# Output projection of a cross attention: the first two groups' values and the weight blocks change places

## The chip, the cores and the metric

The kernel runs on one core of a Trainium2 chip. The metric is the time on the device, in microseconds, as the median of several executions. TensorE (PE) multiplies matrices, VectorE (DVE), ScalarE (ACT) and GpSimd (POOL) work on rows, and SyncE (SP) issues every DMA of this kernel from one queue, in program order.

## The reference, cut to what matters

The reference is one transformer layer with cross attention, self attention and a feed-forward part, in float32. This case is about the end of the cross attention: the heads' outputs (`out`) times `w_o`, plus the bias and the residual, over 2048 rows. The self attention that comes next uses `w_attn` and `w_proj`.

```
out = jnp.einsum('bhij,bhjd->bhid', attn, v)
out = out.transpose(0, 2, 1, 3).reshape(B, Sq, INNER)
return out @ w_o + b_o
...
x = x + _L0_xattn_ref(_layernorm(x, axis=-1), ctx_768, ...)
x = x + _L0_attn_ref(_layernorm(x, axis=-1), L0_attn_w_attn, L0_attn_w_proj, L0_attn_decay_raw)
```

## The kernel before

Products are made in near float32 precision: every factor is split into a high part (a rounding copy, on ACT) and a low part (the factor minus its high part, on DVE or POOL), and each product is three matmuls (high by high, high by low, low by high). So every factor needs its two splits before TensorE can use it.

The 64 sequences are worked in eight groups (`NG`). For each group the attention leaves its values in `o_dram`. When the last sequence has been mixed, TensorE projects the values of group 7 (four steps, `project_values`; ACT copies half of each, `half_value`, DVE adds the other half, `whole_value`, SP stores them, `store_values`). Meanwhile the output projection is made ready. Its parts, which the steps below name, are these:

- `load_out(g)` on SP loads the values of group g, 1 MB, into `o_in[g % 2]`; `high_out` (ACT, L524) and `low_out` (DVE, L529; for half of group 0 POOL) split them into `os_[g % 2]`, in four pieces for each group.
- `load_block(k)` on SP loads weight block k into one of four raw buffers (`w_raw`); `high_block` (ACT, L502) and `low_block` (DVE, L506) split it. Blocks 0 to 7 are `w_o` (the last two, 6 and 7, are split at the end of the attention), blocks 8 to 23 are the weights of the self attention. A load waits until the block that had its buffer is split: from block 12 on, `load_block(k)` waits for `low_block(k - 4)`, and everything behind it in SP's queue waits too.
- TensorE makes two row tiles of each group, 16 in all, 24 matmuls of 128x512 each, into three banks in turn (the accumulate at L1015). The first waits for all eight `w_o` blocks (`w_lo`) and for the split values of its group.
- DVE adds each product to the rows that POOL has given the bias (L801, L1403), and takes their moments (L1405, L1407).
- For the first four row tiles the next stage's norm is made ahead: ACT takes the square root (`ahead.norm.root`, behind the group's `high_block`s in group 2), DVE finishes it beside row tile 4, POOL scales row tile 0, 1, 2, 3 behind the bias of row tiles 5, 7, 9, 11, and TensorE turns them (`ahead.norm.turn`, L167) behind row tiles 6, 8, 10, 12. ACT and DVE split what was turned (L173, L178; on ACT behind the `high_block`s of its group). All four share one bank: a turn waits for the low split of the one before.

`later(g)` names the four blocks whose loads go with group g. Every engine's program is a hand-written order; the compiler moves nothing.

Of the kernel before, what the change touches and what calls it, by code (L numbers as in the profile page):

```python
# [28 lines left out]
DMA = 16  # L29
# [185 lines left out]
def cross_attention(nc, kept, stack, ident, ident_ready, x_rows, w_q, w_k, w_v, w_o, b_o, ctx_dram, q_dram, o_dram,  # L215
# [22 lines left out]
    with Room(nc, "p2") as room:  # L238
# [235 lines left out]

        def later(g):

            return range(KO + g * KT, KO + (g + 1) * KT) if g < 4 else ()

# [10 lines left out]
        def load_block(e, k):  # L491
            if k == 0:
                e.wait_ge(queried, UNITS * NT * NG)
            if last_user(k) is not None:
                e.wait_ge(w_lo, last_user(k) + 1)
            rows = P // len(blocks[k][0])
            for i, source in enumerate(blocks[k][0]):
                e.dma_start(w_raw[buffer(k)][i * rows:(i + 1) * rows, :], source).then_inc(w_in[buffer(k)], DMA)
# [10 lines left out]
        def load_out(e, g):  # L509
            if g >= 2:  # L510
                outs_are_split(e, g - 2)
            if g == NG - 1:
                for i in range(2):
                    e.wait_ge(o_gone[i], DMA * NG * NT // 2)
            e.dma_start(o_in[g % 2][:], o_dram[:, g * GR:(g + 1) * GR].rearrange(
                "(k p) r -> p k r", p=P)).then_inc(o_got[g % 2], DMA)
# [31 lines left out]
        def sync(e):  # L548
# [106 lines left out]
            for g in range(NG + 1):  # L655
                for kind, t, _ in steps[g]:
                    if kind == "o":
                        store_values(g - 1, t)
                    elif t == 0:
                        load_queries(g, NQB)  # L660
                for b in range(g * GB, (g + 1) * GB if g < NG else 0):
                    for j in ffn_block_of(b - 1) if b % GB > 0 else ():
                        store_ffn_block(j)
                    if b + 2 < B:
                        load_context(b + 2)
                    for j in ffn_block_of(b + 1) if b % GB == 0 else ffn_block_of(b) if b % GB > 1 else ():
                        load_ffn_block(j)
                    if b + 2 < B:
                        if b % GB > 0:
                            load_blocks(b + 2)  # L670
                        load_odd(b + 2)
                    if b % GB == GB - 2 and g + 1 < NG:
                        e.wait_ge(ffn_out, 2 * DMA * min((g + 1) * PER_GROUP, len(ffn_blocks)))
                        load_queries(g + 1, 0)
                    if b % GB == GB - 1 and g + 1 < NG:
                        load_queries(g + 1, 1)
                        load_queries(g + 1, 2)
                        load_blocks(b + 3)
                    if g == NG - 1 and b % GB < EARLY:
                        load_block(e, b % GB)  # L680
                if g == NG - 1:
                    e.wait_ge(mixed, KC * B)
                    load_out(e, 0)
                    for k in range(EARLY, KO):
                        load_block(e, k)


            def load_rows(n):
# [3 lines left out]
                e.dma_start(x1s[n % 3][:], x_rows[n * P:(n + 1) * P, :]).then_inc(x1_got[n % 3], DMA)  # L692

            e.wait_ge(valued, 2 * NT * NG)
            e.wait_ge(o_gone[0], DMA * NG * NT // 2)
            load_out(e, 1)
            load_rows(0)
            e.dma_start(bias[:], b_o[None, :].to_broadcast([P, C])).then_inc(bias_in, DMA)
            load_rows(1)
            for g in range(NG):  # L700
                for k in later(g):
                    load_block(e, k)
                if g + 2 < NG:
                    load_out(e, g + 2)
                for n in range(g * NX, (g + 1) * NX):
                    e.wait_ge(added, n + 1)
                    e.dma_start(x1_dram[n * P:(n + 1) * P, :], x1s[n % 3][:]).then_inc(x1_gone[n % 3], DMA)
                    if n + 2 < NG * NX:
                        load_rows(n + 2)
                    if n in loaded_at:  # L710
                        i = loaded_at[n]
                        e.wait_ge(x1_gone[i % 3], DMA * (i // 3 + 1))
                        if i >= 3:
                            e.wait_ge(ahead.norm.chain, i - 2)
                        e.dma_start(ahead.xs[i % 3][:], x1_dram[i * P:(i + 1) * P, :]).then_inc(ahead.x_in[i % 3], DMA)
# [307 lines left out]
        def scalar(e):  # L1023
# [124 lines left out]
            for g in range(NG + 1):  # L1148
                for kind, t, j in steps[g]:
                    if kind == "o":  # L1150
                        half_value(g - 1, t, j)
                    else:
                        high_query(g, t, j)
                    if g == NG and t == 1:
                        for k in range(EARLY, KO):
                            high_block(e, k)
                        for i in range(KO // 2):
                            high_out(e, 0, i)
                if g == NG:
                    break  # L1160
                for b in range(g * GB, (g + 1) * GB):
                    first, second, last = b == g * GB, b == g * GB + 1, b == (g + 1) * GB - 1
                    high_context(b)
                    if second:
                        high_probs(b - 1, 0)
                    elif not first:
                        high_probs(b - 1, 1)
                    exponent(b, 0)
                    if second:
                        high_probs(b - 1, 1)  # L1170
                    for c in turned_in(b):
                        high_turned(c, 0)
                    for tile in range(1, NT):
                        exponent(b, tile)
                    for c in turned_in(b):
                        high_turned(c, 1)
                    if not first:
                        high_mix(b - 1, 0)
                        high_probs(b, 0)
                    if last:  # L1180
                        high_probs(b, 1)
                    if not first:
                        high_mix(b - 1, 1)
                        high_mix(b - 1, 2)
                    if last:
                        high_mix(b, 0)
                        for c in turned_behind(b):
                            high_turned(c, 0)
                        high_mix(b, 1)
                        for c in turned_behind(b):  # L1190
                            high_turned(c, 1)
                        high_mix(b, 2)
                    if g == NG - 1 and 1 <= b % GB <= EARLY:
                        high_block(e, b % GB - 1)
# [14 lines left out]
        def vector(e):  # L1209
# [124 lines left out]
            for g in range(NG + 1):  # L1334
                for kind, t, j in steps[g]:
                    if kind == "o":
                        whole_value(g - 1, t, j)
                    else:
                        low_query(g, t, j)
                    if g == NG and t == 1:  # L1340
                        for k in range(EARLY, KO):
                            low_block(e, k)
                        for i in range(KO // 4):
                            low_out(e, 0, i, os_lo)
                if g == NG:
                    break
                for b in range(g * GB, (g + 1) * GB):
# [48 lines left out]
            for g in range(NG):  # L1396
                if g + 1 < NG:
                    for i in range(KO // 2):
                        low_out(e, g + 1, i, os_lo)
                for n in range(g * NX, (g + 1) * NX):  # L1400
                    e.wait_ge(put, n + 1)
                    e.wait_ge(biased, n + 1)
                    e.tensor_tensor(x1s[n % 3][:], b_x1[n % 3], x1s[n % 3][:], ALU.add).then_inc(added, 1)  # L1403
                    e.wait_ge(added, n + 1)
                    e.bn_stats(x1_stats[n % 2][:], x1s[n % 3][:]).then_inc(x1_seen, 1)  # L1405
                    e.wait_ge(x1_seen, 2 * n + 1)
                    e.bn_aggr(moments[:, n, :], x1_stats[n % 2][:]).then_inc(x1_seen, 1)  # L1407
                    if n == ahead.early - 1:
                        e.wait_ge(x1_seen, 2 * (n + 1))
                        ahead.norm.guard(e, 0)  # L1410
                    if n == ahead.early:
                        ahead.norm.finish(e, 0)
                    if n - 1 in turned_at_tile:
                        ahead.norm.low(e, turned_at_tile[n - 1], *ahead.place(turned_at_tile[n - 1]))
                for k in later(g):
                    low_block(e, k)

        with nc.Block() as block:  # L1418
            block.tensor(tensor)
# [780 lines left out]
```

## Time and profile before

| | |
|---|---|
| median of 3 runs | 1621.39 us (1619.94 to 1623.33) |
| the profiled execution, its time | 1620.81 us |
| its span | 1618.8 us |
| TensorE busy | 1584.7 us, 98% |
| the output projection | from 894.91 us to 985.39 us of the span |
| clock granted to TensorE | 0.995 of full speed |

TensorE is busy for nearly the whole span, so only its idle time, and what ends it, can be won. The times of rows are microseconds from the start of the span.

### The profile page before, as it was taken

Reading aid. Unit: us, or ns where it says so; the run is one execution under the profiler, and the core shown is the slowest. Engines: PE = TensorE matmul, PEld = TensorE weight load, DVE = VectorE, ACT = ScalarE, POOL = GpSimd, SP = SyncE. Lnnn points to the kernel's source line nnn. Section 1 sums busy time; section 2 is a strip of 40 time slices with the busy share of each in tenths; the row PEclk is TensorE's granted clock in tenths of the full one; section 3 lists DMA queues with packets and bytes.
Section 4 is the critical chain, followed back from the end, with each engine's and each line's share of the span. In section 5 each row is a group of like instructions: output and inputs, shape, how many; then the busy total and the mean of one; then the engine's idle time right before and its main releaser. Section 6 shows DMA issues by size and latency. Waiting matters only on the chain. (4 is left out here: it accounts for less than half of the span.)

```text
span 1618.8 us, 30327 instructions
## 1 busy us (share of the span) xinstructions
PE 1584.7 (98%) x11178; PEld 1386.2 (86%) x11178; DVE 1215.7 (75%) x2387; ACT 1016.7 (63%) x2019; POOL 820.6 (51%) x778
## 2 busy tenths in 40 slices
PE   9999999999999999999999999999997999999997
PEld 7879899998999999899999788988986888787886
DVE  5558888887887888888887783656654878788887
ACT  3357777777777777777776532445344666666665
POOL 3317657475674847656363341333333555555554
PEclk9999999999999999999999999999998999999999
DMA  8974636365463655634453864011117501010010
GB/s 251 292 223 147 183 117 181 118 191 158 128 184 116 188 146 147 182 110 132 122 136 89 284 228 131 21 48 53 60 62 252 189 14 59 21 52 20 7 52 26
DMA packets 191746, 207.19 MB, mean 128 GB/s; under 512 B 82480, under 2 KB 139888, under 8 KB 191600
## 3 DMA queue, kind: packets, MB, share of 16 engines
q1 hardware_dynamic: 191600, 205.27, 42.3%
q8 instruction: 89, 1.46, 0.4%
q14 instruction: 57, 0.47, 0.1%
HBM read 150.68 MB, written 54.53 MB: 127 GB/s over the span
## 5 line engine op out<-in xcount | busy, mean ns | idle before, releaser
L75 PE MATMUL p_bank_score<-p_ctxt,p_qo 128*128 128x256 f32 x2304 | 304.5, 286 | 0.7 <-ACT p_probs L1061 0.3
L75 PEld LDWEIGHTS p_bank_score<-p_ctxt,p_qo 128*128 128x128 f32 x2304 | 288.1, 191 | 5.8 <-issue 2.1
L75 PE MATMUL p_bank_mix<-p_probt,p_ctx 128*128 128x512 f32 x1152 | 292.0, 397 | 0.5
L75 PEld LDWEIGHTS p_bank_mix<-p_probt,p_ctx 128*128 128x128 f32 x1152 | 207.4, 189 | 41.8 <-issue 3.7
L2002 POOL TENSOR_TENSOR p_pieces<-p_pieces 128x512 f32<-128x512 f32 x64 | 112.1, 1752 | 152.8 <-ACT p_pieces L2067 152.8
L2033 PE MATMUL p_bank_down<-p_w,p_ht 128*128 128x512 f32 x768 | 186.1, 391 | 2.9 <-DVE p_ht L2111 2.7
L1267 DVE SCALAR_TENSOR_TENSOR p_qo<-p_bank_mix,p_odd,p_qo 128x512 fp32r<-128x512 f32 x192 | 143.8, 749 | 57.7 <-ACT p_qo L1075 50.1
L1075 ACT ACTIVATE p_qo<-p_bank_mix,p_odd 128x512 fp32r<-128x512 f32 x192 | 132.3, 689 | 68.2 <-PE p_bank_mix L75 67.8
L2033 PEld LDWEIGHTS p_bank_down<-p_w,p_ht 128*128 128x128 f32 x768 | 143.5, 188 | 36.7 <-DVE p_ht L2111 4.0
L1061 ACT ACTIVATE p_probs<-p_bank_score,p_small 128x257 f32<-128x257 f32 x256 | 121.3, 475 | 59.5 <-DVE p_small L1248 55.5
L755 POOL TENSOR_SCALAR p_probs<-p_probs,p_small 128x256 f32<-128x256 f32 x256 | 121.3, 480 | 70.5 <-DVE p_small L1254 70.3
L749 POOL TENSOR_TENSOR p_ctx<-p_ctx_in,p_ctx 128x768 fp32r<-128x768 f32 x64 | 118.3, 1848 | 65.4 <-ACT p_ctx L1050 65.0
L744 POOL TENSOR_TENSOR p_ctx_in<-p_ctx_in,p_odd_in 128x768 f32<-128x768 f32 x64 | 118.2, 1846 | 41.9 <-DMA p_odd_in<-in_ctx_dram 41.9
L1248 DVE TENSOR_REDUCE p_small<-p_bank_score 128x1 f32<-128x257 f32 x256 | 105.3, 414 | 10.7 <-PE p_bank_score L75 7.9
L75 PE MATMUL p_bank_mm<-p4a_zt,p_wattn 128*128 128x256 f32 x768 | 96.1, 285 | 3.3 <-PEq L1418 2.0
L75 PEld LDWEIGHTS p_bank_mm<-p4a_zt,p_wattn 128*128 128x128 f32 x768 | 92.9, 191 | 4.9 <-issue 2.4
L1238 DVE SCALAR_TENSOR_TENSOR p_ctxt<-p_bank_turn,p_odd_minus,p_ctxt 128x256 fp32r<-128x256 f32 x192 | 87.0, 481 | 12.1 <-ACT p_ctxt L1040 11.7
L2005 POOL TENSOR_TENSOR p_pieces<-p_pieces,p_rest 128x512 f32<-128x512 f32 x64 | 87.4, 1366 | 9.2
L1040 ACT ACTIVATE p_ctxt<-p_bank_turn,p_odd_minus 128x256 fp32r<-128x256 f32 x192 | 83.5, 470 | 10.5 <-DVE p_bank_turn L1232 8.3
L732 POOL CAST p_qo<-p_probs 128x512 fp32r<-128x512 f32 x32 | 19.5, 610 | 134.8 <-ACT p_probs L1098 134.8
L1232 DVE STREAM_TRANSPOSE p_bank_turn<-p_blocks_in 128x256 f32<-128x256 f32 x192 | 78.6, 440 | 3.2 <-DMA p_blocks_in<-in_ctx_dram 2.9
L2070 ACT ACTIVATE p_ht<-p_m,p_minus 128x512 fp32r<-128x512 f32 x64 | 46.4, 724 | 48.5 <-DVE p_m L2133 48.5
(277 smaller groups left out, 3654.1 us busy)
## 6 DMA issues: line engine op xcount, KB each, us to landing
p_blocks_in<-in_ctx_dram SPq DMA_DIRECT2D x256, 96.0 KB, 2.5
p_ctx_in<-in_ctx_dram SPq DMA_DIRECT2D x64, 384.0 KB, 3.2
q<-p_ctx SPq DMA_DIRECT2D x64, 256.0 KB, 3.6
ffn<-p_w_raw SPq DMA_DIRECT2D x64, 256.0 KB, 3.1
p_odd_in<-in_ctx_dram SPq DMA_DIRECT2D x64, 192.0 KB, 3.8
p_x<-in_x_dram SPq DMA_DIRECT2D x32, 256.0 KB, 4.3
p_quad<-q SPq DMA_DIRECT2D x32, 256.0 KB, 3.6
p_probt<-q SPq DMA_DIRECT2D x32, 256.0 KB, 3.8
```

The costliest lines, as they stand in the source:

```text
L75: made = e.matmul(out, lhsT, rhs, start=n == 0, stop=n == last)
L744: e.tensor_tensor(ctx_in[b % 2][:], ctx_in[b % 2][:], odd_in[:, None, :].to_broadcast([P, SP, CC]), ALU.subtract).then_inc(shifted, 1)
L749: e.tensor_tensor(ctx[b % 2][:, LO], ctx_in[b % 2][:], f32(ctx[b % 2][:, HI]), ALU.subtract).then_inc(ctx_lo, 1)
L755: e.tensor_scalar(probs[n % 6][:, 0:KEYS], probs[n % 6][:, 0:KEYS], small[n % 4][:, 2:3], 1.0, ALU.mult, ALU.mult).then_inc(normal, 1)
L1061: e.activation(probs[n % 6], b_score[n % NS][:, 0:S], ACT.Exp, bias=small[n % 4][:, 0:1], accum_out=small[n % 4][:, 1:2]).then_inc(exped, 1)
L1075: e.activation(qo[:, HI, m, b % GB, :, :].rearrange("p h t -> p (h t)"), b_mix[m], ACT.Identity, bias=odd[:, m, b:b + 1]).then_inc(out_hi, 1)
L1238: e.scalar_tensor_tensor(out=ctxt[b % 2][:, LO, k, :], in0=b_turn[:, (k % 2) * KEYS:(k % 2 + 1) * KEYS], scalar=odd_minus[:, k, b:b + 1], ...
L1248: e.tensor_reduce(small[n % 4][:, 0:1], b_score[n % NS][:, 0:S], AX, ALU.max, negate=True).then_inc(topped, 1)
L1267: e.scalar_tensor_tensor(out=lo, in0=b_mix[m], scalar=odd[:, m, b:b + 1], in1=f32(hi), op0=ALU.add, op1=ALU.subtract).then_inc(out_lo, 1)
L2002: e.tensor_tensor(a[:], a[:], g0[:], ALU.subtract).then_inc(sloped, 1)
L2005: e.tensor_tensor(a[:], a[:], w[:], ALU.mult).then_inc(scaled, 1)
L2033: made = e.matmul(b_down[i], lhsT, rhs, start=f == 0 and j == 0, stop=f == KF - 1 and j == 2)
```

## The change

On SP the load of group 1's values goes up, behind the loads of blocks 6 and 7, and no longer waits for a store of group 7. In each group the load of the values two groups on now goes ahead of the four weight blocks. On ACT and DVE the first group's values are split ahead of blocks 6 and 7. On DVE the low splits of the self attention's blocks move from the end of a group to the middle of the next one, behind that group's `low_out`s and ahead of its row tiles. ACT's order after the first group stays.

```diff
         def later(g):
-            return range(KO + g * KT, KO + (g + 1) * KT) if g < 4 else ()
+            return range(KO + g * KT, KO + (g + 1) * KT) if 0 <= g < 4 else ()
@@ sync
                     load_out(e, 0)
                     for k in range(EARLY, KO):
                         load_block(e, k)
+                    load_out(e, 1)
...
             e.wait_ge(valued, 2 * NT * NG)
-            e.wait_ge(o_gone[0], DMA * NG * NT // 2)
-            load_out(e, 1)
             load_rows(0)
             e.dma_start(bias[:], b_o[None, :].to_broadcast([P, C])).then_inc(bias_in, DMA)
             load_rows(1)
             for g in range(NG):
+                if g + 2 < NG:
+                    load_out(e, g + 2)
                 for k in later(g):
                     load_block(e, k)
-                if g + 2 < NG:
-                    load_out(e, g + 2)
@@ scalar
                     if g == NG and t == 1:
+                        for i in range(KO // 2):
+                            high_out(e, 0, i)
                         for k in range(EARLY, KO):
                             high_block(e, k)
-                        for i in range(KO // 2):
-                            high_out(e, 0, i)
@@ vector
                     if g == NG and t == 1:
+                        for i in range(KO // 4):
+                            low_out(e, 0, i, os_lo)
                         for k in range(EARLY, KO):
                             low_block(e, k)
-                        for i in range(KO // 4):
-                            low_out(e, 0, i, os_lo)
@@ vector
                 if g + 1 < NG:
                     for i in range(KO // 2):
                         low_out(e, g + 1, i, os_lo)
+                for k in later(g - 1):
+                    low_block(e, k)
                 for n in range(g * NX, (g + 1) * NX):
...
-                for k in later(g):
-                    low_block(e, k)
```

On DVE, from the last values of group 7 to group 1's row tiles, the order before is this (`p_wo_late` are blocks 6 and 7, `p_o<-p_o_in` is `low_out`, `p_wattn` are the self attention's blocks):

```order
L1275 TENSOR_TENSOR p_probs<-p_bank_probt,p_probs 64x512
L506 TENSOR_TENSOR p_wo_late<-p_w_raw,p_wo_late 128x512 x2
L529 TENSOR_TENSOR p_o<-p_o_in,p_o 128x512 x2
L1275 TENSOR_TENSOR p_o_out<-p_bank_turn,p_o_out 64x512
...
L1403 TENSOR_TENSOR p_x_1<-p_bank_score,p_x_1 128x512
L1405 BN_STATS p_x_stats<-p_x_1 128x6
L1407 BN_AGGR x_moments<-p_x_stats 128x2
L506 TENSOR_TENSOR p_wattn<-p_w_raw,p_wattn 128x512 x4
L529 TENSOR_TENSOR p_o<-p_o_in,p_o 128x512 x4
L1403 TENSOR_TENSOR p_x_2<-p_bank_score,p_x_2 128x512
```

And in the changed kernel:

```order
L1274 TENSOR_TENSOR p_probs<-p_bank_probt,p_probs 64x512
L529 TENSOR_TENSOR p_o<-p_o_in,p_o 128x512 x2
L506 TENSOR_TENSOR p_wo_late<-p_w_raw,p_wo_late 128x512 x2
L1274 TENSOR_TENSOR p_o_out<-p_bank_turn,p_o_out 64x512
...
L1404 TENSOR_TENSOR p_x_1<-p_bank_score,p_x_1 128x512
L1406 BN_STATS p_x_stats<-p_x_1 128x6
L1408 BN_AGGR x_moments<-p_x_stats 128x2
L529 TENSOR_TENSOR p_o<-p_o_in,p_o 128x512 x4
L506 TENSOR_TENSOR p_wattn<-p_w_raw,p_wattn 128x512 x4
L1404 TENSOR_TENSOR p_x_2<-p_bank_score,p_x_2 128x512
```

The two splits have changed places at both spots; the second exchange is repeated in groups 2, 3 and 4.

On SP, from the end of the attention to group 0's first row tile, the order before is this (`p_o_in<-o` is `load_out`):

```order
L515 DMA p_o_in<-o 128x8x256
L498 DMA p_w_raw<-in_L_xattn_w_o_dram 64x512 x4
L615 DMA o<-p_o_out 128x2x256
L615 DMA o<-p_probs 128x2x256
L615 DMA o<-p_o_out 128x2x256
L615 DMA o<-p_probs 128x2x256
L515 DMA p_o_in<-o 128x8x256
L692 DMA p_x_0<-in_x_dram 128x512
L698 DMA p_bias<-in_L_xattn_b_o_dram 128x512
L692 DMA p_x_1<-in_x_dram 128x512
L498 DMA p_w_raw<-in_L_attn_w_attn_dram 128x512 x4
L515 DMA p_o_in<-o 128x8x256
```

And in the changed kernel:

```order
L515 DMA p_o_in<-o 128x8x256
L498 DMA p_w_raw<-in_L_xattn_w_o_dram 64x512 x4
L515 DMA p_o_in<-o 128x8x256
L615 DMA o<-p_o_out 128x2x256
L615 DMA o<-p_probs 128x2x256
L615 DMA o<-p_o_out 128x2x256
L615 DMA o<-p_probs 128x2x256
L693 DMA p_x_0<-in_x_dram 128x512
L697 DMA p_bias<-in_L_xattn_b_o_dram 128x512
L693 DMA p_x_1<-in_x_dram 128x512
L515 DMA p_o_in<-o 128x8x256
L498 DMA p_w_raw<-in_L_attn_w_attn_dram 128x512 x4
```

The second load of values has moved ahead of the four stores, and the third ahead of the four weight blocks.

## Rows read from the trace of the kernel before

**Rows 1.** The page, part 1: busy time of TensorE, its share, instructions.

```profile
PE 1584.7 (98%) x11178; PEld 1386.2 (86%) x11178; DVE 1215.7 (75%) x2387; ACT 1016.7 (63%) x2019; POOL 820.6 (51%) x778
```

**Rows 2.** Waits of PE, 894 to 987 us: total, times, longest.

```profile
PE p_bank_score L75 <- issue: 1.3, 1, 1.3
PE p_bank_score L75 <- DVE p_o L529: 0.7, 1, 0.7
```

**Rows 3.** Timeline of PE: start, duration, instruction, idle before it.

```profile
894.91 4.35 PE L75 MATMUL p_bank_score<-p_wo_early,p_o 128*128 128x512 f32 x18 [1.33 <-issue]
...
906.75 4.39 PE L75 MATMUL p_bank_score<-p_wo_early,p_o 128*128 128x512 f32 x18 [0.70 <-DVE p_o L529]
...
934.11 0.60 PE L167 MATMUL p_bank_turn<-ident,p4a_z 128*128 128x128 f32 x4
...
945.69 0.60 PE L167 MATMUL p_bank_turn<-ident,p4a_z 128*128 128x128 f32 x4
```

**Rows 4.** Timeline of ACT, 887 to 931 us.

```profile
887.90 0.59 ACT L1085 ACTIVATE p_probs<-p_bank_probt 64x512 f32<-64x512 f32 x1 [0.31 <-PE p_bank_probt L912]
889.02 0.63 ACT L502 ACTIVATE p_wo_late<-p_w_raw 128x512 fp32r<-128x512 f32 x1 [0.53 <-DMA p_w_raw<-in_L_xattn_w_o_dram]
889.88 0.63 ACT L502 ACTIVATE p_wo_late<-p_w_raw 128x512 fp32r<-128x512 f32 x1 [0.23 <-DMA p_w_raw<-in_L_xattn_w_o_dram]
890.42 2.18 ACT L524 ACTIVATE p_o<-p_o_in 128x512 fp32r<-128x512 f32 x4
...
902.44 2.19 ACT L524 ACTIVATE p_o<-p_o_in 128x512 fp32r<-128x512 f32 x4 [7.38 <-DMA p_o_in<-o]
...
928.72 1.28 ACT L148 ACT_TABLE_LOAD   x1
930.01 0.21 ACT L148 ACTIVATE p4a_ln_std<-p4a_ln_safe 128x4 f32<-128x4 f32 x1
```

**Rows 5.** Timeline of POOL: the first group's low splits, row tile 0 scaled.

```profile
892.16 2.65 POOL L529 TENSOR_TENSOR p_o<-p_o_in,p_o 128x512 fp32r<-128x512 f32 x2 [17.55 <-ACT p_o L524]
...
931.40 0.76 POOL L156 TENSOR_SCALAR p4a_z<-p4a_x,p4a_ln_minus,p4a_ln_inv 128x512 f32<-128x512 f32 x1 [4.77 <-DVE p4a_ln_inv L140]
```

**Rows 6.** Timeline of DVE, 903 to 944 us.

```profile
903.10 3.60 DVE L529 TENSOR_TENSOR p_o<-p_o_in,p_o 128x512 fp32r<-128x512 f32 x4 [7.01 <-ACT p_o L524]
...
909.82 2.46 DVE L506 TENSOR_TENSOR p_wattn<-p_w_raw,p_wattn 128x512 fp32r<-128x512 f32 x4
912.20 4.69 DVE L529 TENSOR_TENSOR p_o<-p_o_in,p_o 128x512 fp32r<-128x512 f32 x4
...
931.14 0.69 DVE L1403 TENSOR_TENSOR p_x<-p_bank_score,p_x 128x512 f32<-128x512 f32 x1
...
943.01 0.66 DVE L178 TENSOR_TENSOR p4a_zt<-p_bank_turn,p4a_zt 128x512 fp32r<-128x512 f32 x1
```

**Rows 7.** Timeline of SP's queue: when it issued.

```profile
882.14 0.39 SPq L515 DMA_DIRECT2D p_o_in<-o  x1
882.57 2.51 SPq L498 DMA_DIRECT2D p_w_raw<-in_L_xattn_w_o_dram  x4
887.32 0.38 SPq L615 DMA_DIRECT2D o<-p_o_out  x1
...
896.86 0.36 SPq L515 DMA_DIRECT2D p_o_in<-o  x1
...
922.41 1.85 SPq L498 DMA_DIRECT2D p_w_raw<-in_L_attn_w_attn_dram  x4
```

**Rows 8.** Issue to landing: `load_out(0)`; store of 887.32; blocks 12 to 15; blocks 16 to 19.

```profile
DMA to landing us min/median/max: 5.9/5.9/5.9
...
DMA to landing us min/median/max: 3.1/3.1/3.1
...
DMA to landing us min/median/max: 2.9/4.7/5.4
...
DMA to landing us min/median/max: 3.1/3.9/4.2
```

## Prediction

> **What bounds the kernel now.** I read the page's busy times first: TensorE works for 1584.7 of 1618.8 us, 98% [rows 1]. So time can only come out of its idle time, and go into new idle time of it. The change touches the output projection alone, so the next view is the list of what TensorE waited for there. It names two waits, 1.3 us and 0.7 us [rows 2]. The timeline puts them in place: the first row tile begins at 894.91 after 1.33 us without work, the third at 906.75 after 0.70 us [rows 3]. Between and behind these the products follow each other without a gap. That is the whole prize: 2.0 us of 1621, 0.13%. A measurement of this kernel tells about 0.2% from no change, 3.2 us. The sum below is made against the profiled execution, 1620.81 us with a span of 1618.80; it is 0.6 us under the median of 1621.39, to which I carry the difference over.
>
> Who ends the first wait is called "issue" in that row, which names nobody. I read it off the engines. POOL splits the second half of group 0's values from 892.16 for 2.65 us, until 894.81 [rows 5], 0.1 us before the first product. POOL's start hangs on ACT's four `high_out`s, from 890.42, and these stand behind blocks 6 and 7, whose copies at 889.02 and 889.88 each waited for a DMA [rows 4]. The values had been issued at 882.14 and took 5.9 us, so they were there at 888.04 [rows 7, 8], and ACT had finished its previous work at 887.90 + 0.59 = 888.49 [rows 4]. So ACT idled and copied weights while values lay ready. The second wait is ended by DVE's `low_out`s of group 1. They waited for ACT at 902.44, and ACT for the load issued at 896.86 [rows 4, 6, 7].
>
> **The change, step A: the first product starts earlier.** ACT now begins `high_out` at 888.5. It takes 2.18 us, to 890.7 [rows 4]. POOL began 892.16 - 890.42 = 1.74 us behind ACT's first piece, so it begins at 890.2 and is through at 892.9. Blocks 6 and 7 follow on ACT, 0.6 us each, both landed long before: 890.7 to 891.9. DVE needs about 0.6 us for each of their low splits (four took 2.46 us [rows 6]), so 892.6 if it is left alone. TensorE is occupied with group 7's values until 894.91 - 1.33 = 893.58. Left alone, it would begin at about 893.5, a gain of 1.4 us.
>
> It isn't left alone. DVE's four splits took 2.46 us with POOL quiet, 3.60 us when POOL was at work in part of them and 4.69 us when POOL did two operations beside them [rows 6]: each POOL operation costs DVE about 1.1 us. Before, POOL's two splits met DVE's adds for group 7; now they meet the splits of blocks 6 and 7. One such wait makes 892.6 into 893.7, two make it 894.8. Worked out in turn (POOL's first to about 891.8, then block 6, POOL's second to 893.6, then block 7) it is 894.2. I take 894.2: a gain of 0.7 us, between 0 (two full waits) and 1.4.
>
> The Trainium skill speaks against this part of the change: "SBUF — State Buffer", section "SBUF: two separate sides", says that a DVE operation with two inputs in SBUF and a GpSimd operation exclude each other for a whole instruction. By that rule the low splits of blocks 6 and 7 queue with POOL's and the gain is 0.7; without it, it would be 1.4. The trace agrees (2.46 against 3.60 and 4.69 us [rows 6]).
>
> **Step B: the wait of 0.70 us goes.** `load_out(1)` is issued behind the four pieces of blocks 6 and 7, at 882.57 + 2.51 = 885.1 instead of 896.86 [rows 7]. What is now behind it is the store of group 7's first step, issued at 887.32, and ACT's third step of group 7 waits for that store to leave its buffer. The store took 3.1 us [rows 8], to 890.4. With 1 MB ahead of it, which I price at about 3 us (load_out(0) took 5.9 us including its way), it lands near 893.5, 1.5 us after ACT would ask for it, and the next store similarly. So ACT does group 7's last halves to about 896.3, `high_out` of group 1 to 898.5, DVE `low_out` to about 899.8. TensorE asks for them at 894.2 + 2 x 5.47 = 905.1 (five row tiles lie in 934.11 - 906.75 = 27.4 us, so 5.47 each [rows 3]). 5 us to spare, so a bound of nothing for this part; the gap is gone, -0.70 us. After A and B TensorE is 1.4 us ahead (0.7 to 2.1), and would want to turn the next stage's first row tile at 932.7 instead of 934.11 [rows 3].
>
> **Step C: the turn of row tile 0 becomes late.** This is what the later weight splits cost, through three queues. Take group 1. SP now issues `load_out(2)` ahead of blocks 8 to 11, about 899.5, and the blocks until 902.1. All land by about 908.2. ACT splits the blocks to 908.9 and the values to 911.1. DVE's `low_out(2)` ends at about 913.4 with two POOL operations beside it, and only then come the low splits of blocks 8 to 11, to 915.9. SP can issue blocks 12 to 15 only as these are done, 914.1 to 916.3; ACT has copied them at 919.6 and group 3's values at 921.8. DVE's `low_out(3)` ends between 922.4 and 923.5, and the low splits of blocks 12 to 15 between 925.0 and 927.1 (one more POOL operation or none in each). So SP issues the last of blocks 16 to 19 between 926.0 and 927.1, where before all four were issued from 922.41 for 1.85 us [rows 7], until 924.3. The shortest landing was 3.1 us [rows 8], which I take as DMA has less to do then: 929.1 to 930.2. ACT copies it (0.6 us) and takes the root, which stands behind it in ACT's order: table load and root took 930.22 - 928.72 = 1.5 us [rows 4], so 931.3 to 932.4. From there to the scaled row tile it was 932.16 - 930.22 = 1.94 us [rows 4, 5]. Sum: the turn can be made between 933.3 and 934.4. TensorE would ask for it at 932.7. Before, it was made at 934.11, with 1.95 us to spare behind the scaling at 932.16. So 1.95 us of slack is eaten from two sides: TensorE comes earlier, the root later. I take the middle, 933.9: TensorE is 0.2 us ahead of before, bounds -0.8 and +0.3.
>
> **Step D: the turn of row tile 1 becomes late too.** It stands two products further on: 945.69 - 934.11 = 11.58 us [rows 3], so TensorE asks at 945.5. It shares the bank of the first turn, so it waits for the low split of that, which ended at 943.01 + 0.66 = 943.67 before [rows 6], 2.0 us to spare. ACT's high split of it stands behind blocks 20 to 23. From the root at 931.9: DVE finishes the norm (1.0 us), adds row tile 5 and takes its moments (1.5 us, from 931.14 on before), 934.4; `low_out(4)` 2.46 + 1.1 for POOL, 938.0; low splits of blocks 16 to 19 2.46 + 1.1, 941.6. The last of blocks 20 to 23 can be issued then and lands 3.1 us later, 944.7; ACT's copy 0.6, its high split of the turned rows 0.6, DVE's low split 0.66: 946.6. That is 0.9 us later than 945.69. If POOL stays clear of DVE in both, 944.4, and TensorE is not held (-0.2 remains); with two POOL operations in both, 948.8, +3.1.
>
> Behind that no weight blocks are left: groups 5 to 7 have the order of before. No block copy stands in front of the later turns any more. Nothing is given back either, as everything behind follows TensorE.
>
> **Sum.** -0.7 (A) - 0.7 (B) + 1.2 (C) + 1.1 (D) = +0.9 us. 1620.81 + 0.9 = 1621.7 for the profiled execution, 1621.39 + 0.9 = 1622.3 us for the median.
>
> **The rivals.** (1) *No new wait; both gaps close.* It needs blocks 16 to 19 to be issued as early as before, about 922 to 924. For it: DVE's order delays them only by one `low_out`, and values now land earlier, so that DVE may run ahead. Against it: 1.95 us of slack, of which TensorE's own lead takes up to 1.4. Time: -1.3 to -2.1 us, 1619.3 to 1620.1. Chance 0.25. (2) *Nothing happens*: DVE and POOL hold each other fully at the start, and DVE's wait is the only gain, -0.7, and C and D take it back: 1620.7 to 1621.4. Chance 0.15. (3) *Clearly slower*, the other side: SP stands blocked in front of a weight block. Block loads can take 5.4 us instead of 3.1 [rows 8], since values are now in front of them in the queue. That adds 2.3 us to C and again to D: +0.9 + 4.6 = +5.5 us, 1626.9. It decides once the last of blocks 16 to 19 lands behind 932.5 or the last of 20 to 23 behind 947. For it: the queue moved 1 MB in some 3 us, and one such load stands directly in front. Against it: by the walk it was issued 3 us ahead of the first block. Chance 0.12. The forecast itself, a new wait of TensorE at one or both turns that about cancels the gain (-0.6 to +3), has 0.48.
>
> **How the numbers follow.** All cases but (3) lie inside 0.2%. The range takes in (1) with half a microsecond more, since runs of one kernel lay 3.4 us apart, and most of (3): 1618.6 to 1626.0; the likeliest case alone has 1620.8 to 1624.5. Slower by over 0.2% (over 1624.6) takes (3) less a little, 0.10; faster by over 0.2% (under 1618.2) can't come from 2.0 us of idle time, only from the spread, 0.04; the same, 0.86.
>
> **What the changed profile would show.** A: first product at 894.2 (893.5 to 894.9), ACT's `high_out` at 888.5, ahead of the two weight copies, and one or both DVE splits of `p_wo_late` stretched from 0.7 to 1.8 us. B: no wait of PE for `p_o L529`. C: ACT's table load for the root at 930 or later instead of 928.72, and a wait of PE in front of L167 that names POOL's `p4a_z`. D: a second one, for DVE's `p4a_zt`, of about 1 us. In SP's queue blocks 16 to 19 go out two to three microseconds later. I would be wrong if the turns show no wait (then it is rival 1), or if a product itself waits, for values or for `added`: the walk leaves 2 to 3 us there.

## The result: slower by 0.4%, and the profile after

The changed kernel takes 1628.22 us (median of 5 runs, 1627.07 to 1630.68) against 1621.39 us. The ratio is 1.0041, with a 95% interval from 1.0027 to 1.0055. I had forecast 1622.3 us, with 1626.0 as the upper end: the sign was right, the size was not, and the range didn't hold it. The profiled execution took 1627.07 us, its span is 1625.2 us.

The list of what TensorE waited for, from 894 to 990 us, answers to [rows 2]:

```profile
PE p_bank_turn L167 <- POOL p4a_z L156: 6.5, 1, 6.5
PE p_bank_score L75 <- DVE p_o L529: 1.1, 2, 0.7
PE p_bank_score L75 <- DVE p_wo_late L506: 0.4, 1, 0.4
```

The timeline of PE answers to [rows 3]:

```profile
893.77 4.42 PE L75 MATMUL p_bank_score<-p_wo_early,p_o 128*128 128x512 f32 x18 [0.41 <-DVE p_wo_late L506]
...
916.23 4.38 PE L75 MATMUL p_bank_score<-p_wo_early,p_o 128*128 128x512 f32 x18 [0.36 <-DVE p_o L529]
...
928.15 4.37 PE L75 MATMUL p_bank_score<-p_wo_early,p_o 128*128 128x512 f32 x18 [0.75 <-DVE p_o L529]
932.36 1.52 PE L75 MATMUL p_bank_score<-p_wo_late,p_o 128*128 128x512 f32 x6
940.36 1.09 PE L167 MATMUL p_bank_turn<-ident,p4a_z 128*128 128x128 f32 x4 [6.48 <-POOL p4a_z L156]
941.10 5.53 PE L75 MATMUL p_bank_score<-p_wo_early,p_o 128*128 128x512 f32 x18
...
953.27 0.61 PE L167 MATMUL p_bank_turn<-ident,p4a_z 128*128 128x128 f32 x4
...
995.05 8.86 PE L75 MATMUL p_bank_mm<-p4a_zt,p_wattn 128*128 128x256 f32 x72 [2.01 <-PEq L1417]
```

The first product begins 1.1 us earlier and the wait before the third is gone. Two later products wait for values instead, 0.36 us for group 2 and 0.75 us for group 3, which the prediction had named as a sign of being wrong. And the turn of row tile 0 comes at 940.36 instead of 934.11, after 6.48 us without work. And what follows is slow: the turn takes 1.09 us instead of 0.60, and 18 matmuls 5.53 us instead of some 4.3. The next stage's first product, 987.39 before, starts at 995.05: 7.7 us later at the end of this stage, of which 6.4 us are left in the span.

The timeline of ACT answers to [rows 4]:

```profile
888.30 2.20 ACT L524 ACTIVATE p_o<-p_o_in 128x512 fp32r<-128x512 f32 x4
890.40 1.13 ACT L502 ACTIVATE p_wo_late<-p_w_raw 128x512 fp32r<-128x512 f32 x2
894.52 0.60 ACT L1084 ACTIVATE p_o_out<-p_bank_turn 64x512 f32<-64x512 f32 x1 [2.99 <-DMA o<-p_o_out]
...
908.33 2.59 ACT L502 ACTIVATE p_wattn<-p_w_raw 128x512 fp32r<-128x512 f32 x4 [9.14 <-DMA p_w_raw<-in_L_attn_w_attn_dram]
...
923.31 0.63 ACT L502 ACTIVATE p_wattn<-p_w_raw 128x512 fp32r<-128x512 f32 x1 [0.48 <-DMA p_w_raw<-in_L_attn_w_attn_dram]
...
935.47 1.28 ACT L502 ACTIVATE p_wattn<-p_w_raw 128x512 fp32r<-128x512 f32 x2 [1.13 <-DMA p_w_raw<-in_L_attn_w_attn_dram]
936.77 1.28 ACT L148 ACT_TABLE_LOAD   x1
938.06 0.20 ACT L148 ACTIVATE p4a_ln_std<-p4a_ln_safe 128x4 f32<-128x4 f32 x1
```

The root's table load comes at 936.77 instead of 928.72, directly behind the copies of blocks 16 to 19, which waited for their DMA. The timelines of DVE and of SP's queue show why these came late:

```profile
891.04 2.67 DVE L506 TENSOR_TENSOR p_wo_late<-p_w_raw,p_wo_late 128x512 fp32r<-128x512 f32 x2 [0.72 <-ACT p_wo_late L502]
...
911.47 4.70 DVE L529 TENSOR_TENSOR p_o<-p_o_in,p_o 128x512 fp32r<-128x512 f32 x4 [2.91 <-ACT p_o L524]
916.09 2.48 DVE L506 TENSOR_TENSOR p_wattn<-p_w_raw,p_wattn 128x512 fp32r<-128x512 f32 x4
...
924.50 3.60 DVE L529 TENSOR_TENSOR p_o<-p_o_in,p_o 128x512 fp32r<-128x512 f32 x4 [2.63 <-ACT p_o L524]
928.02 3.58 DVE L506 TENSOR_TENSOR p_wattn<-p_w_raw,p_wattn 128x512 fp32r<-128x512 f32 x4
```

```profile
900.39 2.92 SPq L498 DMA_DIRECT2D p_w_raw<-in_L_attn_w_attn_dram  x4
...
916.80 2.67 SPq L498 DMA_DIRECT2D p_w_raw<-in_L_attn_w_attn_dram  x4
...
929.82 2.13 SPq L498 DMA_DIRECT2D p_w_raw<-in_L_attn_w_attn_dram  x4
```

The reader is to follow one round. DVE splits blocks 8 to 11 from 916.09; SP, which stood in front of `load_block(12)`, issues from 916.80 to 919.47; ACT has copied the last of blocks 12 to 15 at 923.31 + 0.63 = 923.94 and only then splits group 3's values; DVE follows with its part to 928.10, and from 928.02 splits blocks 12 to 15. Each link had stood waiting for the one before it (DVE 2.63 us for ACT's splits). One round takes 928.02 - 916.09 = 11.9 us, while TensorE needs 2 x 5.45 = 10.9 us for the two row tiles of a group. In SP's queue blocks 16 to 19 go out at 929.82, where before it was 922.41 [rows 7].

### The profile page after: what moved, and what is told of

The parts are those of the page before. It is cut to its first block and busy times, and to the rows that moved or that the text cites. A ratio compares the mean times of both kernels' runs of the same rounds, so it can differ in the third digit from the quotient of the medians.

```text
span 1625.2 us, 30326 instructions
## 1 busy us (share of the span) xinstructions
PE 1586.2 (98%) x11178; PEld 1387.0 (85%) x11178; DVE 1217.0 (75%) x2387; ACT 1015.9 (63%) x2019; POOL 820.7 (50%) x778
```

## The experiments

The theory: the moved low splits close a loop (DVE's low split frees a raw buffer, SP loads it, ACT copies it, ACT and then DVE split the values, DVE's low split), and the root and the first turned rows stand at its end. Rivals: the loads' new order on SP (a block now lands behind 1 MB of values), and DVE and DMA being too full anyway. In each run the ratio is to the kernel before on the same chip.

**The start of the change alone.** On the kernel before: the two orders at the start, and the early load.

```diff
+                    load_out(e, 1)          # behind load_block(6), load_block(7)
...
-            e.wait_ge(o_gone[0], DMA * NG * NT // 2)
-            load_out(e, 1)
...
+                        for i in range(KO // 2):
+                            high_out(e, 0, i)
                         for k in range(EARLY, KO):
                             high_block(e, k)
-                        for i in range(KO // 2):
-                            high_out(e, 0, i)
```

(and the same for the low splits on DVE.)

> The kernel before with the start of the change alone: group 0's values split ahead of weight blocks 6 and 7, and group 1's load issued behind those blocks. Splits and loads of the later blocks stay as before. Theory (the low splits of the later blocks, moved behind the values' splits, close a loop DVE - SP - DMA - ACT that makes the root late): both gaps of 1.33 and 0.70 us mostly go, TensorE comes to the first turn some 1.5 us earlier than 934.11 and finds it ready but for 0 to 0.5 us, so 1.0 to 1.8 us faster than before, about 1620. Rival (the early load, in front of the stores and row loads, delays SP and so the block loads): the first turn waits here too, by more than 1 us, and the time is not under before.

Measured: 1621.12 us, ratio 1.0000 (0.9991 to 1.0009). Neither theory had it right: the turn doesn't wait, but no gain is left. The timeline of PE:

```profile
894.20 4.37 PE L75 MATMUL p_bank_score<-p_wo_early,p_o 128*128 128x512 f32 x18 [0.42 <-DVE p_wo_late L506]
...
928.04 4.42 PE L75 MATMUL p_bank_score<-p_wo_early,p_o 128*128 128x512 f32 x18 [0.90 <-DVE p_o L529]
933.81 0.63 PE L167 MATMUL p_bank_turn<-ident,p4a_z 128*128 128x128 f32 x4
941.58 4.38 PE L75 MATMUL p_bank_score<-p_wo_early,p_o 128*128 128x512 f32 x18 [1.66 <-DVE p_o L529]
```

The 1.6 us gained at the start come back, and more, as two waits for values of 0.90 and 1.66 us. The second stands behind the root: DVE's timeline shows it idle for 2.22 us in front of the norm, until ACT's root at 931.50 (1.52 us in the kernel before). The first doesn't, as group 3's values are split ahead of the root. Their load took 9.3 us to land. In the run with the root ahead, below, which has the same orders up to there, it took 7.2 us, and the wait is not seen. So that part looks like a load that landed late in this execution; what delayed it is open.

**The low splits put back.** The changed kernel, its low splits again at the end of their own group:

```diff
-                for k in later(g - 1):
-                    low_block(e, k)
                 for n in range(g * NX, (g + 1) * NX):
...
+                for k in later(g):
+                    low_block(e, k)
```

> The changed kernel with DVE's low splits of the later blocks put back to the end of their own group; its loads keep their new order. Theory of the splits: the wait of 6.5 us for the scaled rows goes, the clock stays at full speed, the time is that of the start alone, 1620 to 1621. Rival of the loads' order (each block load now stands behind 1 MB of values and lands later, which makes the root late): most of the wait stays, 4 us or more, and the time is 1625 or more.

Measured: 1621.87 us, ratio 1.0001 (0.9993 to 1.0010). The wait at the turn falls from 6.48 to 1.53 us. With it go 6.5 us of the time (1.0041 against 1.0001), though the loads keep their new order. So that order alone is not what costs.

**The low splits moved, alone.** The kernel before with the opposite of that edit.

> The kernel before with DVE's move of the low splits alone; start and loads as before. Theory of the splits: TensorE waits at the turn of row tile 0 by 4 to 6 us (it comes there 1.4 us later than in the changed kernel, so a little less than 6.5), the clock falls behind it, and the time is 1627 to 1630, at or above the changed kernel, since the start's gain is missing. Rival of the loads' order: no wait over 1 us at the turn, time within 1.5 us of before.

Measured: 1635.51 us, ratio 1.0092 (1.0079 to 1.0104): twice the loss of the changed kernel, and more than I expected. The timeline of PE:

```profile
933.89 5.89 PE L75 MATMUL p_bank_score<-p_wo_early,p_o 128*128 128x512 f32 x18 [5.21 <-DVE p_o L529]
...
946.11 1.09 PE L167 MATMUL p_bank_turn<-ident,p4a_z 128*128 128x128 f32 x4 [4.96 <-POOL p4a_z L156]
```

A product waits for values of group 3, 5.21 us, and the turn waits besides. With the old order of loads `load_out(3)` stands behind `load_block(12)`, and so in the loop too. Whether this is why it costs more, the next run asks.

**The loads' order back.** The changed kernel with the blocks ahead of the values on SP, in the loop over groups:

```diff
-                if g + 2 < NG:
-                    load_out(e, g + 2)
                 for k in later(g):
                     load_block(e, k)
+                if g + 2 < NG:
+                    load_out(e, g + 2)
```

> The changed kernel with SP's loads in the loop as before: four blocks first, the values two groups on behind them. Only the start and the moved low splits are left. With the low splits alone the kernel was 14 us slower, with the loads' new order too 7 us. Theory: a values' load behind a block load that waits for DVE's moved splits puts the values into the loop as well, so the order of loads was worth 6 to 7 us of repair, and the time here is 1632 to 1635. Rival: the 7 us lay in the missing early load of group 1, and the time here is 1626 to 1629.

Measured: 1636.08 us, ratio 1.0095 (1.0081 to 1.0108), 1 us over the upper end that I had expected. The rival is out: once the splits are moved, the loads' new order is a repair worth 8 to 9 us. The start brings no gain here (1.0095 with it, 1.0092 without). The third row below is SP's:

```profile
916.25 2.62 SPq L498 DMA_DIRECT2D p_w_raw<-in_L_attn_w_attn_dram  x4
918.92 0.43 SPq L515 DMA_DIRECT2D p_o_in<-o  x1
...
932.49 2.13 SPq L498 DMA_DIRECT2D p_w_raw<-in_L_attn_w_attn_dram  x4
```

Group 3's values leave at 918.92, in the changed kernel at 911.35. The round from one set of block loads to the next is 16.2 us here, 13.0 us there. (The 11.9 us above are the same round taken at DVE; SP's next load goes out as the first split of the new round ends, and that one ran beside a POOL operation.)

**The root ahead of the copies.** The changed kernel with one exchange on ACT:

```diff
+                if g == 2:
+                    ahead.norm.root(e, 0)
                 for k in later(g):
                     high_block(e, k)
-                if g == 2:
-                    ahead.norm.root(e, 0)
```

> The changed kernel with one edit: ACT takes the root ahead of its copies of blocks 16 to 19 and not behind them. If the wait at the turn is ACT's place of the root behind block copies whose loads come late, the root is taken at about 928 instead of 938, the wait falls from 6.5 us to under 2 us (DVE finishes the norm beside row tile 4, at about 933 to 934), the clock stays at full speed, and the time falls by 5 to 7 us, to about 1621 to 1623; what is then late next is the turn of row tile 1. If the wait is of the rows themselves (row tile 4 or DVE's load), it stays at 4 us or more and the time above 1625.

Measured: 1626.18 us, ratio 1.0024 (1.0014 to 1.0033), 3 us over what I had expected. The wait for the scaled rows falls to 1.20 us, as the theory had it, but only a part of the time goes with it. The timeline of PE names what is late next:

```profile
934.98 0.63 PE L167 MATMUL p_bank_turn<-ident,p4a_z 128*128 128x128 f32 x4 [1.20 <-POOL p4a_z L156]
950.13 1.09 PE L167 MATMUL p_bank_turn<-ident,p4a_z 128*128 128x128 f32 x4 [3.57 <-DVE p4a_zt L178]
```

The second turn waits 3.57 us for the low split of the first turned rows, whose high split stands on ACT behind the copies of blocks 20 to 23. That is step D, one round on.

**Eight raw buffers.** The changed kernel, four more buffers in the space that `wv` leaves free, orders as they are:

```diff
-        carve(third, "rest_of_wv", [P, 2048])
+        w_raw += [carve(third, f"w_raw{i}", [P, C]) for i in range(4, 8)]
...
-            return k % 2 if k < EARLY else (k - EARLY + 2) % 4
+            return k % 2 if k < EARLY else (k - 4) % 4 if k < 12 else (k - 8) % 8
```

(and eight semaphores `w_in`.)

> The changed kernel with eight raw weight buffers for the later blocks instead of four (the other four in space that the value weights leave free): blocks 12 to 15 wait for nobody and blocks 16 to 19 for the splits of blocks 8 to 11, two groups back. Orders of all engines stay as changed. If the wait at the turn comes from the loop low split - free buffer - load - copy - low split, the last copy of blocks 16 to 19 ends near 930 to 932 instead of 936.75, the wait falls from 6.5 to 0 to 2.5 us, the clock stays, and the time is 1619.5 to 1623. If DVE and DMA are simply too full in this stretch, the wait stays at 4 us or more and the time at 1625 or more.

Measured: 1625.02 us, ratio 1.0017 (1.0008 to 1.0026). The copies of blocks 16 to 19 end at 933.17 instead of 936.75, later than expected. The wait falls to 3.75 us, between my two marks, but the time is at the rival's mark of 1625. So the buffers are a part of the loss and not all of it. SP now issues blocks 12 to 15 at 911.99, but blocks 16 to 19 only at 922.49, behind the rows of group 1, and until 926.50. They go out right behind group 3's values (922.01) and take 6.6 to 8.1 us to land, where in the changed kernel it was 3.2 to 4.5; and the root still stands behind their copies. The time also falls by less than the wait, since TensorE worked longer at the low clock:

```profile
936.79 1.09 PE L167 MATMUL p_bank_turn<-ident,p4a_z 128*128 128x128 f32 x4 [3.75 <-POOL p4a_z L156]
937.53 6.81 PE L75 MATMUL p_bank_score<-p_wo_early,p_o 128*128 128x512 f32 x18
```

The 18 matmuls behind the turn took 6.81 us, against 5.53 in the changed kernel and 4.36 before.

**Both.** The changed kernel with eight buffers and the root ahead.

> The changed kernel with eight raw buffers and with ACT's root ahead of its copies of blocks 16 to 19. Each alone left a wait: eight buffers 3.8 us for the scaled rows (the root), the root ahead 3.6 us for the low split of the first turned rows (the loop). If these two links are the whole loss, both waits fall under 0.5 us and the time is that of the start's gain, 1618.5 to 1620.0. If the moved splits cost something else too, it is 1621 or more.

Measured: 1619.49 us, ratio 0.9990 (0.9981 to 0.9999). As expected, both waits are down to 0.5 us or nothing, and the loss is gone. So these two links, the raw buffers and the root's place, are what makes it; DVE and DMA, whose work is the same here, are not simply too full. A smaller cost of the moved splits is not excluded: the kernel with the start and the root ahead, but without them, has 0.9977 (below), and the intervals of the two just overlap.

**The clock.** The changed kernel with needless transposes on TensorE ahead of the first turn, in two lengths:

```diff
                             after_boundary(e, NG, TURN)
+                            for _ in range(60):
+                                e.transpose(b_turn[:, 0:P], ident[:], ident[:])
                         ahead.norm.turn(e, turned_at_tile[n])
```

> The changed kernel with 60 needless transposes of 128 columns on TensorE just ahead of the first turn, into the bank that the turn then overwrites, about 5.4 us of work inside the wait of 6.5 us. It measures what the clock costs behind the wait. In the changed kernel the turn took 1.09 us and the two products behind it 12.2 us instead of 0.60 and 10.9. If the low clock follows from the idle time, it stays at full speed here, the turn still comes at about 940.4, and the time falls by 1.3 to 1.7 us, to about 1626.6. If the slow product has another cause, the time stays within 0.5 us of the changed kernel.

> The changed kernel with 44 needless transposes ahead of the first turn instead of 60, about 4.8 us of work that ends before the scaled rows are there. The 60 kept the clock at full speed, but ended some 1.5 us late, so that the time did not fall. Here the clock stays up (the idle rest is under 2 us) and the turn is not delayed, so 1.3 to 1.7 us less than the changed kernel, 1626.3 to 1627. If the clock's part is not real, 1628.

Measured: 1628.01 us with 60 (ratio 1.0037, 1.0025 to 1.0050) and 1625.55 us with 44 (1.0025, 1.0015 to 1.0035). The times alone don't settle it: both intervals overlap that of the changed kernel, and the second run is faster than I expected. With the 60 the turn came 1.3 us later than in the changed kernel, which took back what they gave: most of that is a product before them, which waited 1.75 us for values instead of 0.75. The profile of that run shows the rest. These are stretches of 2 us with the columns PE, PEld, DVE, ACT, POOL, granted clock, DMA share, GB/s, of the changed kernel and of the one with 60:

```profile
938.00:940.00 2.00, 0.00 (x0) 0.00 (x0) 1.56 (x8) 1.99 (x6) 0.54 (x1) 0.50 0.00 0
```

```profile
938.00:940.00 2.00, 2.00 (x21) 2.00 (x20) 1.43 (x7) 1.99 (x6) 0.38 (x1) 1.00 0.00 0
```

With TensorE idle the granted clock is 0.50, the 1.2 GHz level, as the turn comes; with TensorE at work it is 1.00. From the first turn to the second it is 953.27 - 940.36 = 12.9 us in the changed kernel, 11.35 us with 60 and 12.69 - 1.16 of a wait = 11.5 us with 44. So I put the clock's part of the loss at 1.4 to 1.6 us.

**A version that beats both.** The start of the change, and the root ahead; splits and loads as before.

> The kernel before with the start of the change, and ACT's root ahead of its copies of blocks 16 to 19. With the start alone TensorE waited later for values of groups 3 (0.90 us) and 4 (1.66 us), and nothing was won. The wait for group 4 came from DVE, which sat 2.2 us waiting for the root. If so, the second wait goes and the time is 1.0 to 2.0 us under the start alone, 1619.3 to 1620.3. If DVE is late for its splits beside POOL, the waits stay and the time is within 0.5 us of 1621.1.

Measured: 1618.59 us, ratio 0.9977 (0.9968 to 0.9986), more than expected and the one clear gain of this study. Of all waits in the output projection 0.42 us at the first product is left. To see whose gain it is, two more:

> The kernel before with ACT's root ahead of its copies of blocks 16 to 19 and nothing else. TensorE never waited for a turn there, so if the start's two gaps and the root's place are two separate things, the time is that of before within 0.5 us, 1621 to 1622, and the 3 us of the kernel with both belong to neither alone. If the root's place alone gives them (DVE no longer sits waiting for it), the time is 1618.5 to 1620.

Measured: 1620.39 us, ratio 0.9992 (0.9984 to 1.0001), with both old gaps (1.27 and 0.79 us) still there. Not told from no change.

> The kernel before with the root ahead and the first group's values split ahead of blocks 6 and 7, but without the early load of group 1. If the early load is worth its 0.70 us, this is about 0.7 us slower than the kernel that has it too (0.9977 of before), with a wait of 1 us or more for group 1's values at the third row tile: 0.9980 to 0.9990 of before. If the early load is worth nothing or costs, the two are equal within 0.3 us.

Measured: 1623.04 us, ratio 1.0004 (0.9995 to 1.0012). The early load is worth more than its 0.70 us: without it the third row tile waits 3.57 us.

```profile
908.45 5.97 PE L75 MATMUL p_bank_score<-p_wo_early,p_o 128*128 128x512 f32 x18 [3.57 <-DVE p_o L529]
```

So the parts don't add up one by one. Start alone 1.0000, root alone 0.9992, both 0.9977; the first product of the next stage begins at 988.86, 987.21 and 985.60, against 987.39 before. In that measure the gain is 1.8 us, about what the two gaps of 2.03 us less 0.42 come to. The time fell by 3.7 us with an interval from 2.3 to 5.2; where the rest comes from stays open.

## Why the prediction was wrong, point by point

**What bounds the kernel**: right. TensorE had 2.0 us to win in this stage, and the best version won about that there.

**Step A**: right in its mechanism. `high_out` began at 888.30, and DVE and POOL did hold each other up: the two low splits took 2.67 us together instead of 1.4. One such wait was paid, not one and a half, so TensorE began at 893.77, with 0.41 us of wait. The gain was 0.9 us (1.33 - 0.41) where I took 0.7.

**Step B**: right, the 0.70 us went, and ACT did wait for the store (2.99 us, harmless). But I priced the early load at its 0.70 us. Once step A is made, it keeps away a wait of 3.57 us.

**Step C failed**, in the sizes of its terms. Its wait stands in the sum with +1.2 us; it was 6.48. "Sum: the turn can be made between 933.3 and 934.4" was 940.36. The links were right in kind and order, but nearly every one was too early:

| | measured | I had | over the upper end |
|---|---|---|---|
| blocks 8 to 11 copied | 910.92 | 908.9 | 2.0 |
| `low_out(2)` done | 916.17 | 913.4 | 2.8 |
| blocks 12 to 15 copied | 923.94 | 919.6 | 4.3 |
| `low_out(3)` done | 928.10 | 922.4 to 923.5 | 4.6 |
| blocks 12 to 15 split | 931.60 | 925.0 to 927.1 | 4.5 |
| the root taken | 938.26 | 931.3 to 932.4 | 5.9 |

Most of the lateness comes in at four links, and three of them are loads of blocks. Blocks 8 to 11 took 7.6 to 7.9 us behind the 1 MB of values, where I had them land by 908.2: 2.0 us. In `low_out(2)` I dropped another 0.8 us: the four splits with two POOL operations beside them take 4.7 us from their start [rows 6]. Blocks 12 to 15 landed in 3.5 to 4.2 us, and from the end of `low_out(2)` to their last copy another 1.5 us were lost. For blocks 16 to 19 I took the shortest landing, 3.1 us, because DMA would have less to do then; it was 3.2 to 4.5 us, and this link lost 1.4. What the walk didn't ask is what the links make together. They close a loop, with a round of 11.9 us against TensorE's 10.9, so it can't catch up, and each landing and each POOL operation is paid in full. With the splits put back, blocks 8 to 11 were as late (copied from 908.81 on) and the time was that of before.

**Step D**: swallowed by C in the changed kernel, since TensorE itself came late. With the root ahead it shows, as 3.57 us where the sum has 1.1.

**"Nothing is given back either"**: the stage ends 7.7 us later and the span is 6.4 us longer; which waits of the next stages shrank is not tested. **Not in the prediction at all**: the clock, 1.4 to 1.6 us. I let a wait cost its length. **A product that waits for values**: the walk left "2 to 3 us there", and two of them waited, 0.36 and 0.75 us.

**The rivals.** "Clearly slower" (0.12) named the place, SP standing in front of a weight block, and its 1626.9 us is the nearest of the four. Its reason was only half right. It let blocks 16 to 19 land in 5.4 us; they took 3.2 to 4.5, and the larger part is that they were issued late, at 929.82. Rival 1's premise, these blocks issued at about 922 to 924, holds in the kernel with the start alone (923.50), and no turn waited there, but still nothing was won. The bound on A and B was fair in itself, but I took it for granted that time won early in a stage stays won; with the start alone two waits for values, the larger one behind the root, gave it back.

## What to carry to other kernels

When a split, a copy or a sum is moved later, ask which buffer it frees, and walk the ring once round: what it releases, who loads, who works on it, until you are at the same instruction again. Compare that round with the pace of the bottleneck engine, not the slack at one point. An instruction that is needed soon (here the root for a norm) must not stand behind a copy that waits for a DMA; here neither that exchange nor the better start showed a gain alone (0.9992 and 1.0000), and together they did (0.9977). And a long wait of TensorE can cost more than its length.

## What the runs showed of the hardware that I had not expected

The price of the low clock behind a wait. In the changed kernel, after 6.48 us idle, the granted clock was 0.50 from 938 to 943 us, the turn took 1.09 us instead of 0.60 and the next 18 matmuls 5.53 instead of 4.36. The same was seen behind waits of 3.75 us (eight buffers) and 3.57 us (root ahead), both with a turn of 1.09 us; behind waits of 1.53 us (low splits back) and 2.02 us (44 transposes) the turn took 0.63 us. "TensorE: Matmul & The Clock Gate" of the Trainium skill says, in its section "Part 1: The HAM clock gate", that an idle TensorE falls back to 1.2 GHz; the rows behind the longer waits agree, and the page was there to be used in the forecast.

The price does not follow the length of the wait. From the turn behind the wait to the next turn it took 12.9 us after 6.48 us, 12.8 us after 3.57 us (950.13 to 962.93), and 14.2 us after 3.75 us (936.79 to 950.98), against 11.35 us at the full clock: 1.4 to 2.8 us more. What differs is how long TensorE worked at the low clock. With eight buffers it was from the turn at 936.79 until after 942 us, in the changed kernel from 940.36 until after 943, and with the root ahead from 950.13 to about 953.
